# The first attention windows in another order, the second weight load moved into the feed-forward, and masked blocks of 128 columns

## What is computed

```python
x = x + attention0(layernorm(x))        # 3 heads of 256, softmax over keys, mean of heads, fc
x = x + ternary_ffn(layernorm(x))       # 1024 hidden, weights in -1, 0, 1 times a scale, silu(up) * gate
# the part that the change is in: 16 causal heads of 128
x = layernorm(x) -> q, k, v = x @ W_Q + b_Q, x @ W_K + b_K, x @ W_V + b_V
scores = where(causal, q @ k.T / sqrt(128), -100000.0)
x = x + sum over heads of (softmax(scores) @ v) @ W_O + b_O
x = x + int8_linear(layernorm(x))       # weights and tokens rounded to int8
```

## Time and profile before

| What | Value |
|---|---|
| median of 3 runs | 536.55 us (535.59 to 536.65) |
| profiled execution | 536.18 us, of which the span from first to last instruction is 534.4 us |
| TensorE busy | 515.2 us (96% of the span), 3302 matmuls |
| VectorE busy | 397.7 us (74%) |
| ScalarE busy | 280.4 us (52%) |
| GpSimd busy | 192.4 us (36%) |
| mean granted TensorE clock | 0.991 of full speed |
| chain that ended last | TensorE 84%, VectorE 10%, DMA 2%, ScalarE 2% |

### The profile page before, as it was taken

The page is one execution under the profiler, slowest core; times in us unless marked ns, Lnnn a source line. Parts: engine busy times, 40 slices in busy tenths (PEclk is TensorE's granted clock), DMA queues, the critical chain, the costliest instruction groups (busy, mean ns, idle before and its releaser), DMA issues.

```text
span 534.4 us, 9325 instructions
## 1 busy us (share of the span) xinstructions
PE 515.2 (96%) x3302; PEld 464.6 (87%) x3302; DVE 397.7 (74%) x994; ACT 280.4 (52%) x664; POOL 192.4 (36%) x277
## 2 busy tenths in 40 slices
PE   8999999999999999999999999999999999999972
PEld 7788989899888789999999999999999999999861
DVE  2996887975645878768668768777767787667897
ACT  2444323434445466656656556656565575665552
POOL 1443033424646244324314223412512533222234
PEclk9999999999999999999999999999999999999996
DMA  9900000000000020100200200200200200000002
GB/s 283 351 6 1 2 0 1 2 1 1 1 1 1 0 81 11 69 2 1 80 1 1 81 2 0 81 1 2 79 1 2 80 1 1 1 1 0 2 1 79
DMA packets 8333, 17.52 MB, mean 33 GB/s; under 512 B 480, under 2 KB 6752, under 8 KB 7264
## 3 DMA queue, kind: packets, MB, share of 16 engines
q1 hardware_dynamic: 7200, 15.89, 8.7%
q10 hardware_dynamic: 1088, 1.05, 0.6%
HBM read 15.88 MB, written 1.05 MB: 32 GB/s over the span
## 4 chain that ended last, share of the span: by engine, by line
PE 84%; DVE 10%; DMA 2%; ACT 2%; issue 1%; POOL 1%; SPq 0%; DVEq 0%; ACTq 0%
PE bank L303 20%; PE bank L305 19%; PE bank L304 19%; PE bank L557 6%; PE bank L548 4%; PE bank L547 4%; PE bank L549 3%; PE bank L486 3%; PE bank L485 3%; DMA Wv_sb<-wv 2%; PE bank L496 1%; PE bank L498 1%; DVE XN L1004 1%; DVE SM L1271 1%; PE bank L354 1%
## 5 line engine op out<-in xcount | busy, mean ns | idle before, releaser
L780 ACT ACTIVATE PR<-SM,nmax 128x128 f32<-128x128 f32 (+3 forms) x128 | 71.9, 562 | 100.6 <-DVE nmax L1271 100.4
L1271 DVE CUSTOM_DVE_ANT_0 SM<-bank,causal 128x128 f32<-128x128 f32 (+3 forms) x128 | 60.7, 483 | 18.2 <-PE bank L549 18.2
L945 POOL TENSOR_TENSOR PR<-PR,rec 128x128 f32<-128x128 f32 x32 | 12.9, 402 | 140.1 <-DVE rec L1278 140.1
L1282 DVE TENSOR_TENSOR PT_lo<-bank,PT_hi 128x128 fp32r<-128x128 f32 (+3 forms) x128 | 59.3, 485 | 2.1 <-ACT PT_hi L785 0.3
L785 ACT CAST PT_hi<-bank 128x128 fp32r<-128x128 f32 (+3 forms) x128 | 50.0, 423 | 5.1 <-PE bank L557 4.3
L303 PE MATMUL bank<-XT_hi,W_hi 128*128 128x512 f32 x128 | 50.6, 395 | 0.3 <-DVE XT_lo L1012 0.3
L902 POOL TENSOR_TENSOR E_lo<-E,E_hi 128x512 fp32r<-128x512 f32 x24 | 31.0, 1300 | 54.7 <-DVE E_hi L1083 54.7
L305 PE MATMUL bank<-XT_hi,W_lo 128*128 128x512 f32 x128 | 50.5, 395 | 0.0
L304 PE MATMUL bank<-XT_lo,W_hi 128*128 128x512 f32 x128 | 50.4, 394 | 0.0
L557 PE MATMUL bank<-ident,PR 128*128 128x128 f32 x320 | 46.2, 273 | 1.8 <-DVE PT_lo L1282 0.8
L547 PE MATMUL bank<-K_hi,Q_hi 128*128 128x256 f32 (+2 forms) x128 | 46.5, 364 | 0.0
(11 more groups left out here) (174 smaller groups left out, 1622.9 us busy)
## 6 DMA issues: line engine op xcount, KB each, us to landing
stage<-pack SPq DMA_DIRECT2D x8, 1027.0 KB, 4.9
X<-x SPq DMA_DIRECT2D x2, 512.0 KB, 8.8
wraw<-wupT SPq DMA_DIRECT2D x1, 1024.0 KB, 10.7
wraw<-wgateT SPq DMA_DIRECT2D x1, 1024.0 KB, 12.7
wraw<-wdownT SPq DMA_DIRECT2D x1, 1024.0 KB, 16.3
Wq_sb<-wq ACTq DMA_DIRECT2D x3, 256.0 KB, 5.4
Wk_sb<-wk SPq DMA_DIRECT2D x3, 256.0 KB, 4.6
Wv_sb<-wv SPq DMA_DIRECT2D x3, 256.0 KB, 8.4
```

The lines of the kernel that those rows point to most:

```text
L780: act.activation(PR[:, c, 0:(c + 1) * P], SM[:, c % 2, 0:(c + 1) * P], ACT.Exp, bias=nmax1[:, c:c + 1], scale=-1.0, accum_out=sum1[:, c:c ...
L1271: dve.tensor_tensor_reduce(SM[:, c % 2, 0:n], bank[2 + c % 2][:, 0:n], causal[:, SEQ - n:SEQ], 1.0, HIGHEST, ALU.add, ALU.min, nmax1[:, c: ...
L1282: dve.tensor_tensor(PT_lo[w % 2][:, 0:c + 1, c * P:(c + 1) * P], bank[4 + c % 2][:, 0:(c + 1) * P].rearrange("p (j q) -> p j q", q=P), PT_ ...
```

## The change

Three things change together. First, the first two pairs also run both on half 0 before they run on half 1 (`HALF_OF`, `PAIR_OF`), so half 1 is first used in window 4, by projections that are issued in window 2. Layer norm 5 therefore moves from before window 0 into windows 0 and 1: its statistics are the new steps G0 and G1 of VectorE in window 0, its normalising is G2 in window 1, and its turning is F0 and F1 in window 1, one column block of the 256 each. Both columns use PSUM bank 7 now, so F1 waits until the low part of F0 has been taken out (`xt_lo` at 11). `rstd(5)` stands behind both parts of `normalise(1, ...)` on GpSimd. Windows 0, 1 and 2 get orders of their own: in window 0 the Q projection stands ahead of all and K ahead of T2; in window 2 the O steps stand elsewhere. Second, pair 1's weights are needed sooner: its Q and K parts are made in steps 12 and 13 of the feed-forward, pair 0's output weights in step 6 (which lets the transfer for pair 1 go), and pair 1's V part and output weights in window 0. Its W buffers move in memory for that. Third, the masked blocks are 128 columns wide: three matmuls of scores and three of attend in each window. The zeros are no longer written, and the counts of the semaphores that they used are shifted.

```diff
--- before.py
+++ after.py
@@ orders of the windows @@
-        LAST = {"pe": {WINDOWS - 2: steps("T0 T1 S0 S1 O0 S2 T2 T3 S3 O1"),
+        SPECIAL = {"pe": {0: steps("Q0 T0 T1 S0 K1 T2 T3 S1 S2 A0 S3 V2"),
+                       1: steps("T0 T1 S0 Q0 T2 T3 S1 S2 K1 F0 A0 F1 S3 V2"),
+                       2: steps("T0 T1 S0 T2 T3 O0 S1 Q0 S2 K1 O1 A0 S3 V2"),
...
-                "act": {WINDOWS - 2: steps("T0 T1 S0 S1 T2 S2 T3 W2 S3"),
+                "act": {0: steps("W2 Q0 T0 T1 S0 K1 T2 T3 S1 S2 A0 S3"),
+                        1: steps("T0 T1 W2 S0 Q0 T2 T3 S1 S2 K1 F0 A0 F1 S3"),
...
+                "dve": {0: steps("W2 Q0 T0 T1 S0 K1 T2 T3 S1 G0 S2 R0 G1 S3 A0 R1"),
+                        1: steps("T0 T1 S0 W2 G2 Q0 T2 T3 S1 S2 R0 K1 F0 A0 S3 F1 R1"),
+                        2: steps("T0 T1 S0 W2 T2 T3 O0 S1 Q0 S2 R0 K1 O1 S3 A0 R1"),
...
-        HALF_OF = [b for _ in range(PAIRS - 2) for b in range(HALVES)] + [0, 0, 1, 1]
-        PAIR_OF = [p for p in range(PAIRS - 2) for _ in range(HALVES)] + [PAIRS - 2, PAIRS - 1] * 2
+        HALF_OF = [0, 0, 1, 1] + [b for _ in range(PAIRS - 4) for b in range(HALVES)] + [0, 0, 1, 1]
+        PAIR_OF = [0, 1] * 2 + [p for p in range(2, PAIRS - 2) for _ in range(HALVES)] + [PAIRS - 2, PAIRS - 1] * 2
...
-        LN_BANKS = {0: (0, 1), 1: (6, 7), 2: (0, 1), 3: (0, 1), 4: (0, 1), 5: (6, 7)}
+        LN_BANKS = {0: (0, 1), 1: (6, 7), 2: (0, 1), 3: (0, 1), 4: (0, 1), 5: (7, 7)}
@@ TensorE @@
+            def layernorm_turn_column(j):
+
+                pe.wait_ge(*((ln_norm, 6 * CT) if j == 0 else (xt_lo, 11)))
+                for c in range(CT):
+                    mm = pe.transpose(bank[7][:, c * P:(c + 1) * P], XN[:, c, j * P:(j + 1) * P], ident[:])
+                mm.then_inc(xt_psum, 1)
...
-                n = max((c + 1) * P, 2 * P)
+                n = (c + 1) * P
...
-                pe.wait_ge(t_free, 4 * w + c + 1)
+                if w > 0 or c > 1:
+                    pe.wait_ge(t_free, 4 * w + c - 1)
...
-                if w == 1:
-                    pe.wait_ge(pt_zero, 1)
                 for j in range(CT):
-                    q0 = min(j * P, SEQ - 2 * P)
+                    q0 = j * P
...
                 for j in range(2 * r + 2):
+                    cols = slice(max(2 * r, j) * P, 2 * (r + 1) * P)
...
-            layernorm_turn(5)
             for w in range(WINDOWS):
                 window(w)
@@ GpSimd @@
-            for turned in (PT_hi[1], PT_lo[1]):
-                pool.memset(turned[:, CT - 1, 2 * P:3 * P].bitcast(F32), 0.0)
-                last = pool.memset(turned[:, 1, 0:P].bitcast(F32), 0.0)
...
+                if q == 6:
+                    split_b(0)
+                if q == 13:
+                    split_a(1, 1)
...
                 normalise(w + 1, 0)
                 normalise(w + 1, 1)
+                if w == 0:
+                    rstd(5)
+                if w == 1:
+                    add_bias(5, bo_bc)
...
-            rstd(5)
             normalise(0, 0)
             normalise(0, 1)
-            add_bias(5, bo_bc)
-            split_b(0)
@@ VectorE @@
+                if q == 6:
+                    load_bv(0)
+                    load_b(0)
+                if q in (12, 13):
+                    load_a(1, q - 12)
...
             project_lo(0, 2)
-            ln_statistics(5)
-            ln_variance(5)
             project_lo(1, 0)
             max1(0, 2)
-            dve.wait_ge(xt_psum, 5)
-            ln_normalise(5)
             project_lo(1, 1)
...
+                    elif kind == "G" and c < 2:
+                        ln_statistics(5, 2 * c, 2 * c + 2)
+                        if c == 1:
+                            ln_variance(5)
+                    elif kind == "G":
+                        dve.wait_ge(xt_psum, 5)
+                        ln_normalise(5)
+                    elif kind == "F":
+                        layernorm_lo(5, [c])
...
-                    if loads_v(w) and (kind, c) == (("O", 1) if w == WINDOWS - 8 else ("S", 1)):
+                    if loads_v(w) and (kind, c) == (("O", 1) if w in (6, WINDOWS - 8) else ("S", 1)):
```

More of the change, by code:

```diff
@@ L262, in window_work @@
         def window_work(engine, w):
-            for kind, c in LAST[engine].get(w, ORDERS[engine][w % 2]):
-                if w == 0 and kind == "O":
-                    continue
-                yield kind, c
-        LN_BANKS = {0: (0, 1), 1: (6, 7), 2: (0, 1), 3: (0, 1), 4: (0, 1), 5: (6, 7)}
+            return SPECIAL[engine].get(w, ORDERS[engine][w % 2])
+        LN_BANKS = {0: (0, 1), 1: (6, 7), 2: (0, 1), 3: (0, 1), 4: (0, 1), 5: (7, 7)}
         GF_USES = 2 * H0
@@ L595, in project_out @@
                     pe.wait_ge(wb_pool, p + 1)
-                    pe.wait_ge(z_free, 2 * g + 3)
+                    pe.wait_ge(z_free, 2 * g + 2)
                 elif g == WINDOWS // 2 - 1:
-                    pe.wait_ge(z_free, WINDOWS + 2)
-                pe.wait_ge(o_free, 2 * g + r + (out_bank(g, r) is bank[7]))
+                    pe.wait_ge(z_free, WINDOWS + 1)
+                if g + r == 0:
+                    pe.wait_ge(xt_lo, 12)
+                else:
+                    pe.wait_ge(o_free, 2 * g + r - (out_bank(g, r) is not bank[7]))
                 for i in range(2):
@@ L686, in _, with layernorm_hi @@
             act.dma_start(fcT_sb[:], fcT.rearrange("(k p) o -> p k o", p=P)).then_inc(ld_fc, 16)
-            def layernorm_hi(k):
+            def layernorm_hi(k, columns=range(KD)):
                 b = k % 2
-                act.wait_ge(xt_psum, k + 1)
-                for j, bk in enumerate(LN_BANKS[k]):
+                for j in columns:
+                    bk = LN_BANKS[k][j]
+                    act.wait_ge(xt_psum, k + 1 + (j if k == 5 else 0))
                     act.copy(XT_hi[:, j, half_cols(b)], bank[bk][:]).then_inc(xt_hi, 1)
@@ L1247, in _ @@
                     layernorm_lo(4)
-            dve.memset(PT_hi[0][:, CT - 1, 2 * P:3 * P].bitcast(F32), 0.0).then_inc(t_free, 1)
-            dve.memset(PT_lo[0][:, CT - 1, 2 * P:3 * P].bitcast(F32), 0.0).then_inc(t_free, 1)
             def project_lo(w, which):
@@ L1429, in _ @@
             token_scale(1)
[L1430 removed]
+            dve.wait_ge(o_free, WINDOWS)
             ln_statistics(7, 2, CT)
```

70 lines of the change are left out of this document (31 added, 39 removed).

## The result

The changed kernel takes 539.25 us (median of 4 runs, 538.87 to 539.39), the kernel before in the same comparison 536.21 us (4 runs, 535.59 to 536.65). The ratio is 1.0058, 95% interval 1.0046 to 1.0070: slower by 3.0 us, clear of the scatter. The span of the profiled execution grew from 534.4 to 537.6 us, +3.2.

A forecast was written before the change was run, and what follows sets the result against it. TensorE's queue and its stops at the attention start were taken to bound the kernel. Stops +3.3, narrowing -2.0 and feed-forward +0.1 summed to +1.4 us, forecast 538.0 us; whole range 530.8 to 540.6, likeliest case 536.3 to 540.5.

The forecast's parts named there:

- Stops of windows 0 and 1: TensorE's waits as attention starts, new order played forward: stops 5.5 us against 2.5 with window 2's, +3.3 us in time.
- last rows: Window 1: T3 waits for window 0's last normalised rows, whose reciprocal VectorE finishes at 196.2; stop 0.3 us.
- stop 0.25; from here it never waits: Window 2: T3 waits 0.25 us for the normalised rows; then TensorE has 12 us of work, VectorE some 9.
- Narrowing, -2.0: Scores and attend blocks cut from 256 to 128 columns: 195 blocks at 0.11 instead of 0.122 us, -2.0 us.
- slope: Rival: narrow blocks continue the wider ones' slope to 0.06 us each, 527.9 us; chance 0.08.
- fall-back: Rival: narrow blocks run like plain fp32 products, 0.101 us more each, 559.7 us or up to 64 more; chance 0.08.
- Feed-forward, +0.1: Second weights in the feed-forward: three more VectorE operations delay layer norm 4's last tile, +0.1 us, bounds 0 and 0.5.
- moves do what they can: Rival: the 2.5 us of stops at the attention start go and the new order leaves none, 532.0 us; chance 0.22.
- Half of the stops: Rival: late stops hold, the first two are shorter as VectorE or ScalarE catch up 1 to 2 us, 536 to 537; chance 0.10.

The follow-up runs named there:

- the doublings: First scores trio issued twice in 28 windows: 128-column blocks on the changed kernel, 549.51 us; 256-column blocks on its wide form, 551.09 us.
- wide form: Changed kernel with its masked blocks back at 256 columns, zeros supplied by six small memsets on VectorE: 541.83 us, ratio 1.0105 to the kernel before.

## Why the prediction was right, and where it was off

It said 538.0 us, slower, and 539.25 was measured, 1.25 more. The change itself was forecast as +1.4 us and is +3.0, so that it was off by 1.6; the time came nearer by luck, since the kernel before was 0.34 us below the 536.55 that the forecast started from. By its own steps:

**Stops of windows 0 and 1.** Right in mechanism, place and nearly in size: from start to start K_lo 0.41 (forecast 0.2), V_lo 0.64 (0.6), PT_lo 1.47 (1.65), last rows 0.54 with the T2 ahead of them (0.3), PT_lo and root 0.99 (0.85), XT_lo 1.57 (1.65); 5.6 against 5.25. From the end of V of window 1 to the start of window 2 it is 25.04 us against 21.75 before, +3.3. Window 2 begins 0.13 us later than played. The root's part is shown by putting it earlier (-0.78 in the trace), that of F1's bank by moving F1, that of the statistics and the norm by making them earlier (-1.83 in the trace). The condition that would have made it wrong, last reciprocal of window 0 before 195.5, did not occur: it came at 196.37.

**Window 2, "stop 0.25; from here it never waits".** This is the step whose mechanism failed. The window lasted 0.78 us longer than before, by two stops, 0.47 at T2 and 0.34 at T3. The forecast had T3's and overlooked that T2 stands straight behind S0 now and needs T0's low part as well, which VectorE makes behind the late last reciprocal (208.44). Undoing the order gave back 0.53. The wait of O1 for the bank of O0, and so for `add_bias(5)`, shows only there, not in the changed kernel.

**Narrowing, -2.0.** The pitch of 0.11 was right, the size of the term was not, and this is the largest error, over 1 of the 1.6 us: 0.012 a block was the mean pitch of wide blocks in one attend, 0.122, less 0.11, and the doublings measured 0.118 and 0.113. With that, 195 blocks are worth 1.0 us, and the 156 of the 26 steady windows 0.8. Those windows gave 1.15 (narrow alone on before) and 0.49 (changed kernel against its wide form), 0.007 and 0.003 a block, so 0.005 is good to about half its size. The rivals of slope and fall-back are both excluded. That the weight loads set the pitch is borne out by their rows (last section), but no run kept the weights and narrowed the columns, or the other way round.
**Feed-forward, +0.1.** From the turns of layer norm 4 to the end of V of window 1 it is 19.01 us against 18.91, +0.10, but by two terms. The turns stretch from 1.04 to 1.35 us, since the normalising starts at 161.96 where it started at 161.54 and takes 2.77 us still. The forecast let part of the shift be made up when GpSimd is done; GpSimd wasn't done, but at work beside it until 164.26. And 0.25 come back between the end of the feed-forward (170.56 before, 170.70 after) and the end of that V, 12.44 us against 12.19, where the norm's statistics no longer stand on VectorE: with the norm back in place these are 12.39 us, and the whole stretch 19.17. The forecast had not seen this gain.

**The sum.** By the trace +4.07 from the end of that V to window 3 (37.82 us against 33.75; +3.29 in windows 0 and 1, +0.78 in window 2), +0.10, -0.70, and -0.27 before and behind: +3.2, against +3.3, +0.1 and -2.0. Window 2 and the price of a narrow block missed in the same direction.

**The rival "moves do what they can"** was wrong for this order. It decided at attend of window 0 finding PT_lo within 0.3 us; it waited 1.47. Even with the norm made early and Q first, 2.1 us of stops stay, so 532.0 was not reached by any order tried. "Half of the stops" is excluded by the first two stops, which were not shorter (0.41 and 0.64 against 0.2 and 0.6 forecast). Whether another order of VectorE's low parts (Q_lo behind PT_lo in window 0, for one) would do better wasn't tried.

## What to carry to other kernels

When work is moved past a point where two in-order engines pass results back and forth, play the new order forward operation by operation; it gave six stops within 0.25 us each, where busy shares said that there was room. Play every engine to the end of the disturbance: the stop missed here was in window 2, where the playing had become a sum of work. And a stop removed from the waiting engine comes back at its next meeting with the late one, unless the late one's own work is made less or earlier: moving the steps at which TensorE waits won 0.2, 0.5 and, in window 2, 0.6 us of the start, moving the norm on VectorE and the root on GpSimd 1.8 and 0.8. And take the price of a unit by doubling it in a kernel that is busy there, rather than by the difference of two readings: 0.122 less 0.11 was more than twice the 0.005 measured.
